# A count matrix relaid during the walk that sums it: 8 of 13 strip panels moved by quarters

## Chip, cores and metric

One core of one Trainium2 chip runs one program. The metric is the device time of one execution in microseconds (us). The kernel before took 4571.13 us (median of 3 runs, 4568.84 to 4574.15).

## The reference, cut to what matters

Four graph layers over 3125 nodes of 64 features and 103125 edges (sorted by destination). Layers 0, 2 and 3 are attention layers whose score depends on the two end nodes alone, so parallel edges weigh the same and all that is needed of the edges is how often each pair occurs:

```python
e = leaky_relu(s1[src] + s2[dst], 0.2)
m = segment_max(e, src); ex = exp(e - m[src])
att = ex / segment_sum(ex, src)[src]
h_prime = zeros.at[dst].add(att[:, None] * hW[src])
```

The kernel builds the matrix C[src, dst] of pair counts once (3200 x 3125, f32, in HBM) and layers 0, 2 and 3 read it. Layer 1 works edge by edge. This case is about how C gets to HBM.

## The kernel before, in words

**The walk.** The edges lie in groups of GE = 512, KE = 4 chunks of 128. The columns of C are cut into WN = 157 strips of WD = 20 destination nodes. A step handles one group against one strip, and there are SL = 360 steps, fixed ahead. A slot is the [128, 500] table of one step: row p is the low part of the source number, the 500 columns are 25 source blocks of 20 destinations. Per step:
- ACT (`distance`, L1100, four instructions, and `left`, L1107) makes the one-hot left operand, in four buffers `row_hot`, up to three steps ahead;
- DVE (`hot`, L1370, four compares of 500 columns, f16 in, bf16 out) makes the right operand `col_hot`, two steps ahead;
- PE (L768) multiplies, four matmuls into one bank;
- DVE (`total`, L1382) adds the bank to the running sum of the strip, multiplied by `keep` (0 where a new strip starts), into one of two flush buffers `fbuf` of four slots each.

After four steps SP (`flush`, L426) stores one buffer to `slots` in HBM, 90 flushes in all. `slots` has one row per (partition, step), and a partition's four slots of a flush lie together, 8000 bytes. In the first 17 pairs of flushes SP also stores zeros to `placed` (L434). The sum of a strip is whole in the last slot of its groups; `slot_i[:, w]` (L1342) is the row of `slots` where strip w's sum stands, for each partition.

**The relay, after the walk.** POOL (L637) waits until every flush has landed, then gathers strip after strip with an indirect DMA, [128, 500] each, 256 KB, 16 strips (WIDE) into one of two buffers `win`, ten panels. DVE (L1470) copies a panel in two halves (13 and 12 source blocks) from order strip-block to order block-strip into `relaid`; SP (L440) stores each half to the columns of C, in pieces of 16 x 20 x 4 = 1280 bytes. Between the panels POOL (L644) gathers rows of destinations, one per block of 128 nodes, with three buffers, and DVE (L1474) counts in them (NB = 25 counts, `row_counted`): a search for the first edge of every node. Each search b waits for count b - 3. Before the relay DVE prepares the row search (L1400 to L1416, `rows_ready`), weights (L1420 to L1429) and layer 0's node stage (`norm`, L1438 to L1447, and `proj`, L1455). After it come a few small operations (L1477 to L1490), a barrier over all five engines, and the first loads of C (L463) for layer 0.

Each engine works through its own list in order; semaphores link them. Indirect DMAs go by POOL and its own queue, all others here by SP.

Of the kernel before, what the change touches and what calls it, by code (L numbers as in the profile page):

```python
# [16 lines left out]
P = 128  # L17
N, D, E = 3125, 64, 103125
NB = -(-N // P)
# [17 lines left out]
PV = NB - 1 + -(-N // 512)  # L37
WIDE = 16
assert GN + WN - 1 <= SL and SL % 8 == 0
# [19 lines left out]
class Steps:  # L59
# [5 lines left out]
    def ran(self, ins):  # L65
        ins.then_inc(self.sem, 1)
        self.n += 1
# [23 lines left out]
def build(nc, x_in, src_in, dst_in, dst_before, dst_after, ea64, ea8, ew, w0, a0, gam, bet, wk1, wk2, wk3, wv1, wv2, wv3,  # L91
# [7 lines left out]
    c_cols = c_flat.rearrange("(b p f) o -> p b (f o)", b=NB, p=P)  # L99
    slots = nc.dram_tensor("slots", (P * SL, BW), F32).ap()  # L100
    slots_v = slots.rearrange("(p s) f -> p s f", p=P)
    mask_rows = nc.dram_tensor("mask_rows", (NB, P, N), BF16).ap()
# [9 lines left out]
    with ExitStack() as ctx:  # L112
        def sb(name, shape, dt=F32):
            return ctx.enter_context(nc.sbuf_tensor(name, shape, dt))

        def sem(name):
            return ctx.enter_context(nc.semaphore(name))
# [35 lines left out]
        arena = sb("arena", [P, ARENA])  # L153

        firstc = sb("firstc", [P, 2])
        lowest = sb("lowest", [P, 1])
# [22 lines left out]
        cb = Carve()  # L179
        cb.at = NP  # L180
        dgi, sgi, dgf, blki = (cb(2 * GE, t).rearrange("p (h n) -> p h n", h=2) for t in (I32, I32, F32, I32))
        lowf, keyf = (cb(2 * GE).rearrange("p (h n) -> p h n", h=2) for _ in range(2))
# [7 lines left out]
        chosen = [cb(SL) for _ in range(2)]  # L190
        base20, row0, keep = cb(SL), cb(1), cb(SL)
        last_dst, limit, limit_before, limit_end = cb(2, I32), cb(2), cb(2), cb(2)
        offset, outside, col_key = (cb(KE * SL).rearrange("p (k s) -> p k s", k=KE) for _ in range(3))
        minus_key = offset
        apart = [cb(KE * P, BF16) for _ in range(4)]
        iota16 = cb(COLS, F16)
        row_hot = [cb(KE * P, BF16) for _ in range(4)]
        col_hot = [cb(KE * BW, BF16) for _ in range(4)]
        assert cb.at <= cv.at
        cb.at = NP  # L200
        fbuf = [cb(4 * BW).rearrange("p (s f) -> p s f", s=4) for _ in range(2)]
        assert cb.at <= NP + 4 * 2 * GE
        cb.at = NP
        win = [cb(WIDE * BW) for _ in range(2)]
        relaid = [cb(13 * WIDE * WD) for _ in range(2)]
        assert cb.at <= cv.at
        big_m = cv(NP)
# [16 lines left out]
        tmp_n = sb("tmp_n", [P, NB, D])  # L224
        agg = sb("agg", [P, NB, D + 1])

# [81 lines left out]
        relaid_sb = sem("relaid_sb")  # L308
        relaid_out = [sem(f"relaid_out{i}") for i in range(2)]
        placed_zeroed, placed_out, seed_in = sem("placed_zeroed"), sem("placed_out"), sem("seed_in")  # L310
# [50 lines left out]
        def barrier(eng, k):  # L361

            eng.drain().then_inc(phase, 1)
            eng.wait_ge(phase, 5 * k)
# [6 lines left out]
        def fence(eng, go):  # L373

            eng.sem_inc(go, 1)

        block = ctx.enter_context(nc.Block())

# [8 lines left out]
        def _(sp):  # L387
# [33 lines left out]
            def flush(q, par):  # L421

                sp.wait_ge(summed, q * 4 + 4)
                if not isinstance(q, int):
                    fence(sp, sp_go)
                sp.dma_start(slots_v[:, bass.ds(q * 4, 4), :], fbuf[par]).then_inc(flushed[par], 16)  # L426

            for i in range(SL // 8):
                for par in range(2):
                    flush(i * 2 + par, par)  # L430
                lo = i * CROW
                if lo < W * D:
# [3 lines left out]
            for i in range(-(-WN // WIDE)):  # L436
                n = min(WIDE * WD, N - i * WIDE * WD)
                for half, (lo, nb) in enumerate(((0, 13), (13, 12))):
                    sp.wait_ge(relaid_sb, 2 * i + half + 1)
                    sp.dma_start(c_cols[:, lo:lo + nb, i * WIDE * WD:i * WIDE * WD + n],  # L440
                                 relaid[half][:, 0:nb * WIDE * WD].rearrange("p (b f) -> p b f", b=nb)[:, :, 0:n]).then_inc(relaid_out[half], 16)
            for half in range(2):
                sp.wait_ge(relaid_out[half], 16 * -(-WN // WIDE))
            barrier(sp, 1)
# [182 lines left out]
        def _(pool):  # L627

            for par in range(2):
                pool.wait_ge(flushed[par], 16 * (SL // 8))  # L630
            pool.wait_ge(placed_zeroed, 16 * -(-W * D // CROW))
            pool.wait_ge(table_out, 16)
            for i in range(-(-WN // WIDE)):
                if i >= 2:
                    pool.wait_ge(relaid_sb, 2 * i - 2)
                for w in range(i * WIDE, min(i * WIDE + WIDE, WN)):
                    pool.indirect_dma_start(out=win[i % 2][:, (w % WIDE) * BW:(w % WIDE + 1) * BW], out_offset=None, in_=slots,  # L637
                                            in_offset=bass.IndirectOffsetOnAxis(ap=slot_i[:, w:w + 1], axis=0)).then_inc(win_in[i % 2], 16)
                if i == 1:
                    pool.wait_ge(rows_ready, 1)  # L640
                for b in range(3 * i - 3, min(3 * i, NB)) if i else ():
                    if b >= 3:
                        pool.wait_ge(row_counted, b - 2)
                    pool.indirect_dma_start(out=found[b % 3], out_offset=None, in_=dst_in,  # L644
                                            in_offset=bass.IndirectOffsetOnAxis(ap=row_i[:, b:b + 1], axis=0)).then_inc(row_found[b % 3], 16)
            barrier(pool, 1)

# [648 lines left out]
        def _(dve):  # L1296
# [38 lines left out]
            dve.wait_ge(consts, 16)  # L1335
            ran(V.tensor_scalar(row0, nid[:, 0:1], float(SL), None, ALU.mult))
            ran(V.tensor_copy(out=sel[:, :, :], in_=cst[:, C_SEL:C_SEL + 4 * P].rearrange("p (j m) -> p j m", j=4)))
# [3 lines left out]
            V.tensor_tensor(base20, ps[7][:, 0:SL], iota20[:, 0:SL], ALU.add).then_inc(key_sb, 1)  # L1341
            V.scalar_tensor_tensor(slot_i[:, :], ps[6][:, 0:WN], row0, iota[:, 0:WN], ALU.add, ALU.add).then_inc(key_sb, 1)  # L1342
            dve.wait_ge(key_sb, 2)
# [29 lines left out]
            def total(s, j, n):  # L1373
# [10 lines left out]
                add.then_inc(summed, 1)  # L1384

            hot(0, 0)
            hot(1, 1)
# [3 lines left out]
            for i in range(SL // 8 - 2):  # L1391
                for j in range(8):
                    hot(i * 8 + (10 + j), (j + 2) % 4)
                    total(i * 8 + (8 + j), j, i * 16 + 16)
            for s in range(SL - 8, SL):
                if s + 2 < SL:
                    hot(s + 2, (s + 2) % 4)
                total(s, s % 8, 16 * (SL // 8 - 1))

            ran(V.tensor_scalar(diag0, ident, firstc[:, 0:1], None, ALU.mult))  # L1400
# [15 lines left out]
            do(V.tensor_copy(out=row_i[:, :], in_=row_f))  # L1416
            signal(rows_ready)

            dve.wait_ge(setup_a, 2)
# [37 lines left out]

            node_stage(0, 0)
            dve.wait_ge(brow_sb, NJ)


            for i in range(-(-WN // WIDE)):
                n = min(WIDE, WN - i * WIDE)
                dve.wait_ge(win_in[i % 2], 16 * (WIDE * (i // 2) + n))
                w4 = win[i % 2].rearrange("p (w b d) -> p b w d", w=WIDE, b=NB)
                for half, (lo, nb) in enumerate(((0, 13), (13, 12))):
                    if i:
                        dve.wait_ge(relaid_out[half], 16 * i)
                    o4 = relaid[half][:, 0:nb * WIDE * WD].rearrange("p (b w d) -> p b w d", b=nb, w=WIDE)
                    V.tensor_copy(out=o4[:, :, 0:n, :], in_=w4[:, lo:lo + nb, 0:n, :]).then_inc(relaid_sb, 1)  # L1470
                for b in range(3 * i - 3, min(3 * i, NB)) if i else ():
                    dve.wait_ge(row_found[b % 3], 16 * (b // 3 + 1))
                    at(row_counted, b, dve)
                    V.scalar_tensor_tensor(junk_b, found[b % 3], nid[:, b:b + 1], ones[:, 0:1].to_broadcast([P, W]),  # L1474
                                           ALU.is_le, ALU.mult, accum_out=cnt_in[:, b:b + 1]).then_inc(row_counted, 1)
            dve.wait_ge(row_counted, NB)
            do(V.scalar_tensor_tensor(cnt, row_f, float(W), cnt_in, ALU.mult, ALU.add))  # L1477
# [453 lines left out]
```

## Time and profile before

| | |
|---|---|
| median of the runs | 4571.13 us |
| the profiled execution | 4576.4 us, span 4574.6 us |
| DVE busy | 3821.1 us (84%) |
| PE busy | 3285.9 us (72%) |
| ACT busy | 2136.6 us (47%) |
| POOL busy | 1857.4 us (41%) |
| moved by DMA | 674.27 MB, mean 147 GB/s |
| L637, the strip gathers | x157, 171.6 us busy |
| L1370, the compares | x1440, 404.4 us busy |

Times in the rows are us from the span's start; busy is time in which the engine runs an instruction, and an instruction's duration can overlap the next one's on the same engine. A wait is put down to the event that came last. The walk takes the stretch from about 42 to 685 us, the relay the one from 690 to 973 us.

### The profile page before, as it was taken

How to read it: one execution, taken by the hardware profiler on the slowest of the kernel's cores; microseconds unless marked ns; L12 is line 12 of the kernel's file. 1: busy time of each engine (PE TensorE's matmuls, PEld its weight loads, DVE VectorE, ACT ScalarE, POOL GpSimd, SP SyncE). 2: the span in 40 equal slices, each digit the busy share in tenths (PEclk: the TensorE clock that was granted, in tenths of full speed). 3: DMA queues.
4: the chain of work that ended last, by engine and by line, in shares of the span. 5: the costliest groups of instructions: out<-in, count | busy, mean ns of one | idle time of the engine just before them, and what ended most of it. 6: DMA issues, size and time to landing. Idle time of an engine off the chain costs nothing. (4 is left out here: it accounts for less than half of the span.)

```text
span 4574.6 us, 66771 instructions
## 1 busy us (share of the span) xinstructions
PE 3285.9 (72%) x20105; PEld 1471.8 (32%) x20105; DVE 3821.1 (84%) x6803; ACT 2136.6 (47%) x4380; POOL 1857.4 (41%) x3682
## 2 busy tenths in 40 slices
PE   5555552016639999999994399999999998148166
PEld 2111111001214444444442144444444443122122
DVE  8999994359968888888888788888888886699898
ACT  6999990037723333334332144444444443057066
POOL 0000006720047777777762266666666665100000
PEclk9999995558769999999997699999999999579589
DMA  4653338986625555555551133333333332455544
GB/s 174 256 208 144 144 145 269 365 284 210 197 63 140 149 142 140 145 146 144 142 144 52 34 92 92 92 93 93 93 92 92 92 92 73 140 181 210 173 183 176
DMA packets 359857, 674.27 MB, mean 147 GB/s; under 512 B 71068, under 2 KB 261724, under 8 KB 347856
## 3 DMA queue, kind: packets, MB, share of 16 engines
q1 hardware_dynamic: 319824, 591.23, 39.0%
q0 software_dynamic: 39680, 78.78, 6.3%
q8 instruction: 167, 2.74, 0.3%
q14 instruction: 186, 1.52, 0.1%
HBM read 398.98 MB, written 270.79 MB: 146 GB/s over the span
## 5 line engine op out<-in xcount | busy, mean ns | idle before, releaser
L671 POOL DMA_INDIRECT arena<-h_table,gidx x808 | 785.1, 972 | 306.0 <-issue 229.4
L1635 DVE TENSOR_TENSOR arena<-banks,arena 128x512 f32<-128x512 f32 x808 | 536.2, 684 | 58.5 <-PE banks L861 38.9
L768 PE MATMUL banks<-arena 128*128 128x500 bf16 x1440 | 366.3, 376 | 278.2 <-DVE arena L1370 272.0
L1755 DVE TENSOR_TENSOR arena<-banks,arena 128x512 f32<-128x512 f32 x808 | 518.4, 683 | 37.2 <-PE banks L971 13.1
L1763 DVE TENSOR_TENSOR arena<-banks,arena 128x512 f32<-128x512 f32 x808 | 516.0, 680 | 1.3 <-PE banks L977 1.3
L1100 ACT ACTIVATE arena<-arena 128x128 bf16<-128x128 f16 x1440 | 455.8, 391 | 40.0 <-DVEq L1302 40.0
L637 POOL DMA_INDIRECT arena<-slots,slot_i x157 | 171.6, 1093 | 742.6 <-DMA slots<-arena 689.4
L1235 ACT ACTIVATE arena<-banks 64x256 f32<-64x256 f32 x808 | 306.0, 379 | 340.6 <-PE banks L1003 333.6
L991 PE MATMUL banks<-arena 128*64 128x256 f32 x3232 | 438.6, 392 | 0.5 <-DVE arena L1765 0.5
L977 PE MATMUL banks<-arena 64*128 64x512 f32 x1616 | 436.3, 617 | 0.9 <-DVE arena L1763 0.9
L867 PE MATMUL banks<-arena 128*64 128x256 f32 x3232 | 429.1, 387 | 0.0
L1370 DVE TENSOR_SCALAR arena<-arena 128x500 bf16<-128x500 f16 x1440 | 404.4, 345 | 0.1
L696 POOL TENSOR_TENSOR arena<-arena,same_prev 128x64 f32<-128x64 f32 x808 | 237.3, 294 | 394.4 <-ACT arena L1245 346.9
L819 PE MATMUL banks<-arena,proj 128*65 128x512 f32 (+1 forms) x700 | 277.3, 548 | 89.5 <-DVE arena L1837 89.5
L1171 ACT ACTIVATE arena<-banks 128x512 f32<-128x512 f32 x202 | 120.6, 597 | 404.6 <-PE banks L885 404.6
L867 PEld LDWEIGHTS banks<-arena 128*64 128x64 f32 x3232 | 214.7, 137 | 241.3 <-issue 91.2
L768 PEld LDWEIGHTS banks<-arena 128*128 128x128 bf16 x1440 | 117.4, 97 | 527.2 <-DVE arena L1370 439.9
L697 POOL TENSOR_TENSOR arena<-arena 128x64 f32<-128x64 f32 x808 | 259.2, 321 | 63.5
L819 PE MATMUL banks<-arena,lw 128*64 128x512 f32 (+1 forms) x350 | 182.2, 684 | 133.5 <-DVE lw L1527 133.5
L991 PEld LDWEIGHTS banks<-arena 128*64 128x64 f32 x3232 | 196.0, 136 | 246.0 <-DVE arena L1765 153.3
L1227 ACT ACTIVATE arena<-banks 128x256 f32<-128x256 f32 x202 | 77.6, 384 | 421.3 <-PE banks L993 421.3
L1382 DVE SCALAR_TENSOR_TENSOR arena<-arena,banks 128x500 f32<-128x500 f32 x359 | 263.5, 734 | 7.2 <-PE banks L768 1.0
(289 smaller groups left out, 6399.1 us busy)
## 6 DMA issues: line engine op xcount, KB each, us to landing
arena<-c_flat SPq DMA_DIRECT2D x75, 1562.5 KB, 6.8
slots<-arena SPq DMA_DIRECT2D x90, 1000.0 KB, 3.8
arena<-hs_dump SPq DMA_DIRECT2D x404, 128.0 KB
arena<-mask_rows SPq DMA_DIRECT2D x50, 781.2 KB, 4.3
arena<-in_edge_attr SPq DMA_DIRECT2D x202, 128.0 KB
arena<-placed SPq DMA_DIRECT2D x202, 128.0 KB
xs_dump<-arena SPq DMA_DIRECT2D x202, 128.0 KB
hs_dump<-arena SPq DMA_DIRECT2D x202, 128.0 KB
```

Source lines behind the costliest of these rows:

```text
L671: pool.indirect_dma_start(out=xs[par][:, k * D:(k + 1) * D], out_offset=None, in_=h_table, in_offset=bass.IndirectOffsetOnAxis(ap=gidx[par ...
L768: last = pe.matmul(ps[4 + r % 2][:, 0:BW], row_hot[r][:, k * P:(k + 1) * P], col_hot[r][:, k * BW:(k + 1) * BW], start=k == 0, stop=k == K ...
L819: last = pe.matmul(ps[j][0:rows, 0:n], proj[:, b, 2:rows + 2] if base else lw[par][:, :], ptile[par][:, j * COLS:j * COLS + n], start=b == ...
L867: last = pe.matmul(ps[7][k * D:(k + 1) * D, 0:TW // 2], k3[j], bt[j][:, k * (TW // 2):(k + 1) * (TW // 2)], start=j == 0, stop=j == 3)
L977: pe.matmul(ps[5 + j % 2][:, :], v3[j][rows, :], hv[t % 2][rows, :], start=True, stop=True).then_inc(y_ps, 1)
L991: last = pe.matmul(ps[2][k * D:(k + 1) * D, 0:TW // 2], wo[j], vt[j][:, k * (TW // 2):(k + 1) * (TW // 2)], start=j == 0, stop=False)
L1100: last = act.activation(apart[r % 4][:, k * P:(k + 1) * P], iota16[:, 0:P], ACT.Abs, bias=minus_key[:, k, bass.ds(s, 1)])
L1235: copied = act.activation(xat[r][half * D:(half + 1) * D, k * (TW // 2):(k + 1) * (TW // 2)], ps[0][k * D:(k + 1) * D, 0:TW // 2], ACT.Copy)
L1370: made = V.tensor_scalar(col_hot[r][:, k * BW:(k + 1) * BW], iota16[:, 0:BW], col_key[:, k, bass.ds(s, 1)], None, ALU.is_equal)
L1635: V.tensor_tensor(bt[j], ps[5 + j % 2][:, :], h2k[t % 2], ALU.mult).then_inc(bt_sb, 1)
L1755: V.tensor_tensor(dt_[j % 2], ps[3 + j % 2][:, :], xat[t % 3], ALU.mult).then_inc(dt_sb, 1)
L1763: V.tensor_tensor(vt[j], ps[5 + j % 2][:, :], dt_[j % 2], ALU.mult).then_inc(vt_sb, 1)
```

## The change

- Panels are of 12 strips instead of 16: 13 panels, the last of 13 strips. Each is copied and stored in four quarters of 7, 6, 6 and 6 source blocks, each quarter with its own buffer and semaphore. A stored piece is 12 x 20 x 4 = 960 bytes.
- Panels 0 to 7 are copied and stored during the walk: quarter i of panel g after step 4(58 + 4g + i) + 1, and its store by SP right behind flush 58 + 4g + i.
- POOL gathers three strips of a panel when flush 53 + 4g (then 54 + 4g, 55 + 4g, 56 + 4g) has landed, so panels 0 to 8 fall due within the walk and panel 9 to 12 after it. Panel 8 is copied right after the walk, panel 9 after `rows_ready`, panels 10, 11 and 12 between the counts, and the node stage of layer 0 stands between count 8 and panel 11.
- `slots` has its rows ordered step first, then partition, so that a gather can be bounded to the flushes that have landed; a flush writes four pieces of 2000 bytes per partition. `slot_i` takes two operations instead of one.
- Buffers move: `win` and `relaid` beside `fbuf` and `keep`; `row_hot`, `apart` and one `col_hot` into the space of `brow`; three `col_hot` into that of `big_m`; `offset` and `col_key` into `h` and `agg`.

```diff
-WIDE = 16
+WIDE = 12
+PANELS = WN // WIDE
+INSIDE = 8
+QUARTERS = ((0, 7), (7, 6), (13, 6), (19, 6))
...
-    slots_v = slots.rearrange("(p s) f -> p s f", p=P)
+    slots_v = slots.rearrange("(s p) f -> p s f", p=P)
...
+        def panel(g):
+            lo = g * WIDE
+            n = WIDE if g < PANELS - 1 else WN - lo
+            return lo, n, (GN - 1 + lo + n - 1) // 4
+        def copied_after(g, i):
+            return 4 * (58 + 4 * g + i) + 1
...
+            def store_panel(g, i):
+                lo, n, _ = panel(g)
+                cols = min(n * WD, N - lo * WD)
+                b, nb = QUARTERS[i]
+                sp.wait_ge(relaid_sb, 4 * g + i + 1)
+                sp.dma_start(c_cols[:, b:b + nb, lo * WD:lo * WD + cols],
+                             relaid[i][:, 0:nb * n * WD].rearrange("p (b f) -> p b f", b=nb)[:, :, 0:cols]).then_inc(relaid_out[i], 16)
+            stores = {copied_after(g, i) // 4: (g, i) for g in range(INSIDE) for i in range(4)}
             for i in range(SL // 8):
                 for par in range(2):
                     flush(i * 2 + par, par)
+                    if i * 2 + par in stores:
+                        store_panel(*stores[i * 2 + par])
...
+            def landed(q):
+                pool.wait_ge(flushed[0], 16 * (q // 2 + 1))
+                pool.wait_ge(flushed[1], 16 * ((q + 1) // 2))
+            def gather_panel(g):
+                lo, n, _ = panel(g)
+                if g >= 2:
+                    pool.wait_ge(relaid_sb, 4 * g - 4)
+                for w in range(lo, lo + n):
+                    q = min(max((GN - 1 + lo + n - 1) // 4, 53 + 4 * g + (w - lo) // 3), SL // 4 - 1)
+                    if (w - lo) % 3 == 0:
+                        landed(q)
+                    pool.indirect_dma_start(out=win[g % 2][:, (w - lo) * BW:(w - lo + 1) * BW], out_offset=None, in_=slots[0:(q + 1) * 4 * P, :],
+                                            in_offset=bass.IndirectOffsetOnAxis(ap=slot_i[:, w:w + 1], axis=0)).then_inc(win_in[g % 2], 16)
...
+            for g in range(INSIDE + 3):
+                gather_panel(g)
+            pool.wait_ge(placed_zeroed, 16 * -(-W * D // CROW))
+            pool.wait_ge(table_out, 16)
+            pool.wait_ge(rows_ready, 1)
+            find_rows(0, 3)
+            gather_panel(INSIDE + 3)
+            find_rows(3, 9)
+            gather_panel(INSIDE + 4)
+            find_rows(9, NB)
...
+            def copy_panel(g, i):
+                lo, n, _ = panel(g)
+                dve.wait_ge(win_in[g % 2], 16 * (WIDE * (g // 2) + n))
+                if g:
+                    dve.wait_ge(relaid_out[i], 16 * g)
+                w4 = win[g % 2][:, 0:n * BW].rearrange("p (w b d) -> p b w d", w=n, b=NB)
+                b, nb = QUARTERS[i]
+                o4 = relaid[i][:, 0:nb * n * WD].rearrange("p (b w d) -> p b w d", b=nb, w=n)
+                V.tensor_copy(out=o4, in_=w4[:, b:b + nb, :, :]).then_inc(relaid_sb, 1)
...
                     hot(i * 8 + (10 + j), (j + 2) % 4)
                     total(i * 8 + (8 + j), j, i * 16 + 16)
+                    if i * 8 + 8 + j in copies:
+                        copy_panel(*copies[i * 8 + 8 + j])
...
+            for i in range(4):
+                copy_panel(INSIDE, i)
...
             signal(rows_ready)
+            for i in range(4):
+                copy_panel(INSIDE + 1, i)
...
+            count_rows(0, 6)
+            for i in range(4):
+                copy_panel(INSIDE + 2, i)
+            count_rows(6, 9)
+            node_stage(0, 0)
+            for i in range(4):
+                copy_panel(INSIDE + 3, i)
+            count_rows(9, 15)
+            for i in range(4):
+                copy_panel(INSIDE + 4, i)
+            count_rows(15, NB)
```

`find_rows` and `count_rows` hold the two loop bodies that stood between the panels before (L644, L1474).

## Rows read from the trace of the kernel before

**Rows 1.** Busy us by stretch: PE, PEld, DVE, ACT, POOL; granted clock, DMA share, GB/s

```profile
44.00:50.00 6.00, 4.74 (x12) 1.31 (x12) 4.14 (x14) 6.00 (x18) 0.00 (x0) 0.50 0.00 0
...
460.00:660.00 200.00, 113.94 (x452) 36.66 (x452) 198.08 (x564) 200.00 (x563) 0.00 (x0) 1.00 0.35 145
740.00:960.00 220.00, 0.00 (x0) 0.00 (x0) 84.19 (x67) 0.00 (x0) 157.59 (x147) 0.50 1.03 356
```

**Rows 2.** Timeline, start and duration in us: the walk's last sums, C's first loads

```profile
683.55 1.59 DVE L1382 SCALAR_TENSOR_TENSOR arena<-arena,banks 128x500 f32<-128x500 f32 x2 [1.05 <-PE banks L768]
...
972.94 2.25 SPq L463 DMA_DIRECT2D arena<-c_flat  x4
```

**Rows 3.** Waits from 686 to 1000 us: in total, times, longest

```profile
DVE arena L1470 <- DMA arena<-slots,slot_i: 88.1, 7, 15.4
```

**Rows 4.** Timeline of DVE just after the walk's start

```profile
50.59 0.73 DVE L1382 SCALAR_TENSOR_TENSOR arena<-arena,banks 128x500 f32<-128x500 f32 x1
51.23 1.12 DVE L1370 TENSOR_SCALAR arena<-arena 128x500 bf16<-128x500 f16 x4
...
55.64 0.73 DVE L1382 SCALAR_TENSOR_TENSOR arena<-arena,banks 128x500 f32<-128x500 f32 x1
```

**Rows 5.** Groups by line and shape, 686 to 990 us

```profile
L1470 DVE COPY arena<-arena 128x4160 f32<-128x4160 f32 x9 | 40.4, 4486 | 97.3 <-DMA arena<-slots,slot_i 75.0 <-DMA c_flat<-arena 11.6 <-ACT arena L1086 10.8
L1474 DVE SCALAR_TENSOR_TENSOR arena<-arena,cst,ones 128x808 bf16<-128x808 int32 x25 | 26.5, 1061 | 1.7
...
L1470 DVE COPY arena<-arena 128x3840 f32<-128x3840 f32 x9 | 19.7, 2190 | 33.6 <-DMA c_flat<-arena 33.6
...
L1470 DVE COPY arena<-arena 128x3380 f32<-128x3380 f32 x1 | 2.1, 2054 | 13.1 <-DMA arena<-slots,slot_i 13.1
```

**Rows 6.** Gathers beside DVE: all casts of L1583, then the timeline, twice

```profile
L1583 DVE CAST arena<-arena x26: 411/420/640, 1314.1 to 2339.8; 128x512 bf16<-128x512 f32 x26
...
2143.69 0.95 POOL L671 DMA_INDIRECT arena<-h_table,gidx  x1 [0.30 <-issue]
...
2144.18 0.16 DVE L1629 COPY gidx<-srci 128x4 int32<-128x4 int32 x1
2144.25 0.64 DVE L1583 CAST arena<-arena 128x512 bf16<-128x512 f32 x1
...
860.72 2.16 DVE L1470 COPY arena<-arena 128x3840 f32<-128x3840 f32 x1 [1.94 <-DMA c_flat<-arena]
861.04 2.66 POOL L637 DMA_INDIRECT arena<-slots,slot_i  x1 [0.30 <-issue]
```

**Rows 7.** DMA queues (packets, MB, share of 16 engines) at 300:600, then 760:940

```profile
q1 hardware_dynamic: 6048, 43.01, 34.6%
...
q0 software_dynamic: 8568, 36.23, 53.8%
q1 hardware_dynamic: 23098, 29.26, 50.1%
```

**Rows 8.** The flushes of the walk (59 to 683 us), landing after issue

```profile
DMA to landing us min/median/max: 3.8/3.8/4.2
```

**Rows 9.** The strip gathers: durations, first and last start, landing after issue

```profile
L637 POOL DMA_INDIRECT arena<-slots,slot_i x157: 942/947/3118, 689.8 to 950.1; - x157
...
DMA to landing us min/median/max: 3.4/6.3/11.9
```

**Rows 10.** Timeline of DVE after the walk

```profile
699.55 1.82 DVE L1438 TENSOR_REDUCE stat<-x 128x25 f32<-128x1600 f32 x1
...
726.04 0.43 DVE L1455 COPY proj<-banks 128x264 f32<-128x264 f32 x1 [1.07 <-PE banks L801]
...
964.55 0.18 DVE L1477 SCALAR_TENSOR_TENSOR cnt<-row_f,cnt_in 128x25 f32<-128x25 f32 x1
...
967.80 0.18 DVE L1490 CAST start_i<-cnt 128x25 int32<-128x25 f32 x1
```

More of the change, by code:

```diff
@@ L99, in build @@
     c_cols = c_flat.rearrange("(b p f) o -> p b (f o)", b=NB, p=P)
-    slots = nc.dram_tensor("slots", (P * SL, BW), F32).ap()
-    slots_v = slots.rearrange("(p s) f -> p s f", p=P)
+    slots = nc.dram_tensor("slots", (SL * P, BW), F32).ap()
+    slots_v = slots.rearrange("(s p) f -> p s f", p=P)
     mask_rows = nc.dram_tensor("mask_rows", (NB, P, N), BF16).ap()
@@ L153, in build @@
         arena = sb("arena", [P, ARENA])
+        agg = sb("agg", [P, NB, D + 1])
         firstc = sb("firstc", [P, 2])
@@ L180, in build @@
         cb.at = NP
+        fbuf = [cb(4 * BW).rearrange("p (s f) -> p s f", s=4) for _ in range(2)]
+        iota16 = cb(COLS, F16)
+        keep = cb(SL)
+        panels_at = cb.at
         dgi, sgi, dgf, blki = (cb(2 * GE, t).rearrange("p (h n) -> p h n", h=2) for t in (I32, I32, F32, I32))
@@ L190, in build @@
         chosen = [cb(SL) for _ in range(2)]
-        base20, row0, keep = cb(SL), cb(1), cb(SL)
+        base20, last_step = cb(SL), cb(WN)
         last_dst, limit, limit_before, limit_end = cb(2, I32), cb(2), cb(2), cb(2)
-        offset, outside, col_key = (cb(KE * SL).rearrange("p (k s) -> p k s", k=KE) for _ in range(3))
+        outside = cb(KE * SL).rearrange("p (k s) -> p k s", k=KE)
+        offset, col_key = (v[:, :, :].rearrange("p b f -> p (b f)")[:, 0:KE * SL].rearrange("p (k s) -> p k s", k=KE) for v in (h, agg))
         minus_key = offset
+        assert cb.at <= cv.at
+        cb.at = panels_at
+        win = [cb((WIDE + 1) * BW) for _ in range(2)]
+        relaid = [cb(nb * (WIDE + 1) * WD) for _, nb in QUARTERS]
+        assert cb.at <= cv.at
+        cb.at = 0
         apart = [cb(KE * P, BF16) for _ in range(4)]
-        iota16 = cb(COLS, F16)
         row_hot = [cb(KE * P, BF16) for _ in range(4)]
[L198 to L206, printed above, removed]
+        col_hot = [cb(KE * BW, BF16)]
+        assert cb.at <= NP
+        cb.at = cv.at
+        col_hot += [cb(KE * BW, BF16) for _ in range(3)]
+        assert cb.at <= cv.at + NP
         big_m = cv(NP)
@@ L224, in build @@
         tmp_n = sb("tmp_n", [P, NB, D])
-        agg = sb("agg", [P, NB, D + 1])
         diag0, frow = (agg[:, :, :].rearrange("p b f -> p (b f)")[:, i * P:(i + 1) * P] for i in range(2))
@@ L308, in build @@
         relaid_sb = sem("relaid_sb")
-        relaid_out = [sem(f"relaid_out{i}") for i in range(2)]
+        relaid_out = [sem(f"relaid_out{i}") for i in range(4)]
         placed_zeroed, placed_out, seed_in = sem("placed_zeroed"), sem("placed_out"), sem("seed_in")
@@ L434, in _ @@
                     sp.dma_start(placed_v[:, lo:lo + n], zeros[:, 0:n]).then_inc(placed_zeroed, 16)
[L436 to L443, printed above, removed]
+            for g in range(INSIDE, PANELS):
+                for i in range(4):
+                    store_panel(g, i)
+            for i in range(4):
+                sp.wait_ge(relaid_out[i], 16 * PANELS)
             barrier(sp, 1)
@@ L627, in _, with find_rows @@
         def _(pool):
[L629 to L641, printed above, removed]
+            def landed(q):
[11 more added lines that the diff above has]
+                                            in_offset=bass.IndirectOffsetOnAxis(ap=slot_i[:, w:w + 1], axis=0)).then_inc(win_in[g % 2], 16)
+            def find_rows(lo, hi):
+                for b in range(lo, hi):
                     if b >= 3:
@@ L1335, in _ @@
             dve.wait_ge(consts, 16)
-            ran(V.tensor_scalar(row0, nid[:, 0:1], float(SL), None, ALU.mult))
             ran(V.tensor_copy(out=sel[:, :, :], in_=cst[:, C_SEL:C_SEL + 4 * P].rearrange("p (j m) -> p j m", j=4)))
@@ L1341, in _ @@
             V.tensor_tensor(base20, ps[7][:, 0:SL], iota20[:, 0:SL], ALU.add).then_inc(key_sb, 1)
-            V.scalar_tensor_tensor(slot_i[:, :], ps[6][:, 0:WN], row0, iota[:, 0:WN], ALU.add, ALU.add).then_inc(key_sb, 1)
+            do(V.tensor_tensor(last_step, ps[6][:, 0:WN], iota[:, 0:WN], ALU.add))
+            V.tensor_scalar(slot_i[:, :], last_step, float(P), nid[:, 0:1], ALU.mult, ALU.add).then_inc(key_sb, 1)
             dve.wait_ge(key_sb, 2)
@@ L1384, in total @@
                 add.then_inc(summed, 1)
+            def copy_panel(g, i):
[7 more added lines that the diff above has]
+                V.tensor_copy(out=o4, in_=w4[:, b:b + nb, :, :]).then_inc(relaid_sb, 1)
+            copies = {copied_after(g, i): (g, i) for g in range(INSIDE) for i in range(4)}
+            assert max(copies) < SL
             hot(0, 0)
@@ L1398, in _ @@
                 total(s, s % 8, 16 * (SL // 8 - 1))
+                if s in copies:
+                    copy_panel(*copies[s])
+            for i in range(4):
+                copy_panel(INSIDE, i)
             ran(V.tensor_scalar(diag0, ident, firstc[:, 0:1], None, ALU.mult))
@@ L1456, in node_stage, with count_rows @@
                 dve.wait_ge(proj_sb, 4 * (k + 1))
[L1458 to L1471, printed above, removed]
+            def count_rows(lo, hi):
+                for b in range(lo, hi):
                     dve.wait_ge(row_found[b % 3], 16 * (b // 3 + 1))
@@ L1475, in _ @@
                                            ALU.is_le, ALU.mult, accum_out=cnt_in[:, b:b + 1]).then_inc(row_counted, 1)
+            count_rows(0, 6)
[3 more added lines that the diff above has]
+            node_stage(0, 0)
+            for i in range(4):
+                copy_panel(INSIDE + 3, i)
+            count_rows(9, 15)
+            for i in range(4):
+                copy_panel(INSIDE + 4, i)
+            count_rows(15, NB)
+            dve.wait_ge(brow_sb, NJ)
             dve.wait_ge(row_counted, NB)
```

## The prediction

> **What bounds the kernel now.** First the busy time by stretch [rows 1]. In the walk (about 42 to 685 us) ACT and DVE are both full (200.00 and 198.08 of 200 us) and the DMA engines work at 0.35 once the zeros are written; from 740 to 960 us PE and ACT do nothing, DVE is busy 84 of 220 us, and the DMA engines are full at 356 GB/s. That second stretch is what the count matrix costs after the walk: from the end of the walk's last sum (683.55 + 1.59 = 685.1 us) to the first load of the matrix at 972.9 us [rows 2] it is 287.8 us, nothing of layer 0 can start before it ends, and the longest waits of its copies are for gathers (88.1 us) [rows 3]. So a strip moved while the walk has free DMA time is gained, and what it costs the walk has to be paid on DVE.
>
> Who paces the walk? In steady state ACT runs 562 instructions in its full 200 us [rows 1], five to a step: 1.78 us. Just after the start DVE is behind and runs alone: of four sums in a row the first starts at 50.59 and the last at 55.64, 1.68 us apart each, of which 1.12 go to the compares [rows 4]. So a step costs ACT 1.78 us and DVE 1.68; DVE has 0.10 us a step to give, and ACT, which may be three steps ahead, hides nothing more.
>
> **Part 1: copies in the walk.** 32 quarter copies go in, one per four steps. Prices [rows 5]: 4160 elements took 4.49 us (1.04 ns each behind a fixed 0.15), 3840 took 2.19 (0.52 ns behind 0.19). The slow form has 13 blocks into a target without gaps; the last panel's 3380 elements, also 13 blocks but into a target with gaps, took 2.05, the fast rate. A quarter of 7 blocks (1680 elements, no gaps) is nearest to the slow row: 1.90 us (fast: 1.06); a quarter of 6 (1440) is even like 12: 0.91 us. The Trainium skill (VectorE: DVE Perf Modes, Mode 2×_2P) says two ports serve a copy if the outermost dimensions are both even, or odd and equal; these rows agree, and by it the 7-block quarter is slow too. A panel is 1.90 + 3 x 0.91 = 4.63 us, eight are 37.1 us. From the first copy (after step 233) to step 359 DVE has 127 steps x 0.10 = 12.4 us to give. Net +24.7 us (least, with the 7-block quarter fast, +18).
>
> **Part 2: gathers beside DVE.** In the walk DVE's one-hot compare takes 1.12 of 1.68 us for four times 500 columns [rows 4], about half of what the slow copy needs per element, so it is taken to use both ports. No gather ran beside it; the nearest rows are layer 1's casts beside gathers [rows 6]. A gather began at 2143.69, the cast at 2144.25 took 0.64 us where the median is 0.42 and ended 0.78 + 0.42 us after the gather's start; the small copy that began at 2144.18, 0.49 us after it, took its usual 0.16. So a gather shuts DVE out of the two-port forms from about 0.54 to 0.78 us after its start: 0.24 us at most. With the compare there 1.1 of 1.68 us, a gather costs about 0.64 x 0.24 + 0.01 = 0.165 us; about 108 gathers (panels 0 to 8) fall into the walk: +18 us, between 0 (DVE's queued compares go first) and 26. The other way round, a gather that began at 861.04 under a two-port copy took 2.66 us in place of 0.95: it ended 0.82 us after the copy [rows 6]. Under compares I take one gather per 1.3 to 1.75 us in place of 1.25; three per flush take 4 to 5.2 us, which fits into four steps.
>
> The rule that speaks against the change: the Trainium skill (SBUF — State Buffer, Who interferes with whom) says that the port pair which DVE and GpSimd share is locked for the whole instruction of whoever came first. What the sum would be by it is the second rival below; the copy at 2144.18, inside a gather and not slowed, speaks against it.
>
> **Part 3: transfers in the walk.** Per flush there are now 1.02 MB of flush in pieces of 2000 B (before 8000), 0.77 MB of gathers, and on average 0.77 MB of stores in pieces of 960 B (before 1280). From 760 to 940 us a hardware packet (29.26 MB in 23098, 50.1% of 16 x 180 us) took 62 ns for 1267 B; in the walk (43.01 MB in 6048, 34.6% of 16 x 300 us) 275 ns for 7112 B [rows 7]: 16 ns + 0.036 ns per byte. That makes 2.85 us for the flush, 2.57 for a store and, at the gathers' own 53.8% of 16 x 180 us for 36.23 MB, 2.05 us: 7.5 us. The period is 4 x 1.68 + 1.16 + 3 x 0.165 = 8.4 us. 89% full: it fits, with queueing. A flush landed 3.8 us after issue [rows 8], a gather 3.4 us at least and 6.3 in the median, mostly in the full stretch [rows 9]. Quarter 0 of a panel is copied six steps after the flush that its last three strips need is issued: 6 x (1.68 + 0.14) + 0.91 = 11.8 us. Needed: flush 4.5 to 6, third gather issued 2.5 to 3.5 later, landing 3.4 to 6.3: 10.4 to 15.8 us, middle about 12.8. One us of waiting per panel, +8 us, between 0 and 32. The flush buffers are not late (four steps plus a copy against 4 to 6 us), nor are the targets of the copies (four flushes). SP has nothing else in its queue there, and each store stands behind a flush whose sums come later than the copy. The walk gets **24.7 + 18 + 8 = 51 us** longer (18 to 95).
>
> **Part 4: after the walk.** Left are 49 gathers, 61 strips to store, 25 row searches. Clock from the walk's end, durations as before [rows 5, 9, 10]:
> - panel 8's last gathers (flush 88) land at 4; copied 4 to 9;
> - DVE's set-up (685.1 to 699.5 before, 14.4 us; its search part ends 2 us earlier) 9 to 23; row searches may start;
> - POOL gathers panel 9 from 4 to 24 (12 x 1.25 us, 0.95 and the 0.31 between two [rows 6, 9], held up by the copies and by two-input operations), panel 10 to 41; panel 9 is copied 28 to 33;
> - searches 0 to 2 are issued by 45, counted by 50; panel 11's gathers to 61, searches 3 to 5 counted by 70 (DVE takes its work in order and waits from 35 on, save for the counts); panel 10 copied by 75, counts 6 to 8 by 79;
> - node stage (699.55 to 726.5 before, 27 us) to 106; panel 11 copied by 110, counts 9 to 14 by 120; panel 12 by 125;
> - ten more counts. Search b waits for count b - 3, so three take one landing and one count, 4.5 + 1.2 us: 1.9 us each, to 145. Before, the closing operations took 964.55 to 967.98, 3.4 us, and the load came 5 us later, with the last store, which now has long landed; 3.4 us and the barrier: **150 us**.
> Transfers: 12.5 + 15.6 + 10.3 = 38.4 MB at 356 GB/s are 108 us, so they no longer bind; searches and DVE's order do. Bounds 130 (no wait before the node stage) and 170. Gain 287.8 - 150 = 138 us. The one added operation before the walk costs 0.3 us; slot numbers and buffers moved elsewhere cost nothing.
>
> **Sum.** 51 - 138 = -87 us. The profiled execution took 4576.4 us (span 4574.6); the median of the runs is 5.3 us lower. 4576.4 - 87 - 5 = **4485 us**.
>
> **Rivals.** (a) Nearly all costs absent: locks lost to DVE's queue, no landing late: walk +20, tail 140: about 4443. For it: casts that don't start in that quarter of a microsecond keep their median [rows 6], and a flush landed within 4.2 us at most [rows 8]. 12%. (b) A gather blocks a compare for its whole 0.95 us: 108 x 0.6 x 0.95 = 62 us in place of 18, and later gathers: about 4535. Against it rows 6. 10%. (c) The DMA engines become the bound of the walk: if 960 B pieces and 2000 B pieces cost half as much again, the flush takes 10 us against 8.4, 34 times 1.7 us, and landings are late by 3 us a panel: +82, about 4567. For it: 89% by my own sum. 8%. (d) **Slower**: POOL starves. If a gather has to wait for a gap between the compares twice (once to read its indices, once to write), and each time until the next step, it takes more than two steps. Twelve gathers have 16 steps and four copies, 33 us per panel. A panel's 16 steps took 28.5 us before, so the change loses from 28.5 + 138 / 9 = 44 us per panel on, 3.7 us per gather; at 4 us per gather it is 48 us, +175 us in the walk: about 4608. For it: 1.7 us of delay from a single copy [rows 6]; against it: sums leave 0.6 us of every step free, and the reads come within the first 0.1 us. 4%. (e) The change doesn't do what it says: panels are copied so late that part of the eight still lie behind the walk; each costs there 12 x 1.66 us (157 gathers from 689.8 to 950.1 us [rows 9]): two panels, +40, about 4525. 6%. The forecast itself, 4455 to 4515, has 60%.
>
> A change of PE's clock is no term: from 44 to 50 us the granted clock was 0.50 (1.2 GHz) and 12 matmuls made PE busy for 4.74 us [rows 1], 1.58 us a step and still under 1.68.
>
> **Numbers.** Range 4443 to 4545: it leaves out part of (a), (c) and (d). About 0.2% (9 us) is what a measurement here can tell from no change. Faster 0.93, same 0.02, slower 0.05, from (d), part of (c), and what I haven't seen.
>
> **What the profile would show.** Right: copies of 1680 elements near 1.9 us and of 1440 near 0.9; the walk's period 8.4 us per flush from step 233; compares' mean a few tens of ns up; DMA at 0.9 there; the matrix's first load about 150 us after the last sum; waits of the copies for gathers about 1 us each. Wrong: gathers over 2.5 us in the walk (d), sums waiting for flushes (c), the row searches hiding less or more than the tail above.

## The result, and the profile after

The changed kernel took 4517.38 us (median of 4 runs, 4509.15 to 4524.02) against 4572.64 us (4 runs) before: the ratio is 0.9876, 95% interval 0.9864 to 0.9889, 55 us less. The profiled execution took 4518.56 us, its span is 4516.8. The forecast was 87 us less and 4485 us, with a range of 4443 to 4545.

The trace splits the difference in two. Timeline of the changed kernel, the walk's last sums and the first loads of C, as [rows 2]:

```profile
754.22 1.56 DVE L1428 SCALAR_TENSOR_TENSOR arena<-arena,banks 128x500 f32<-128x500 f32 x2
...
913.80 2.32 SPq L492 DMA_DIRECT2D arena<-c_flat  x4
```

The walk ends at 755.8 us (before 685.1: 70.6 longer, forecast 51), and from there to the first load it is 158.0 us (before 287.8: 129.8 shorter, forecast 138). -130 + 71 = -59 us, and the span is 58 us shorter.

Busy time by stretch, as [rows 1] (the last stretch is the one behind the walk):

```profile
461.00:700.00 239.00, 122.47 (x404) 36.04 (x402) 198.63 (x525) 185.59 (x516) 81.19 (x75) 0.81 0.84 268
...
756.00:914.00 158.00, 27.63 (x101) 19.51 (x101) 75.57 (x115) 7.68 (x15) 84.43 (x77) 0.52 0.88 265
```

From step 233 on the walk no longer fills DVE: 198.63 of 239 us, where it had been full [rows 1]. The missing 40 us stand in the groups of DVE by shape for the same stretch, as [rows 5]: name, count, busy time, mean ns, and idle time before:

```profile
L1416 DVE TENSOR_SCALAR arena<-arena,agg 128x500 bf16<-128x500 f16 x400 | 114.7, 347 | 0.0
L1428 DVE SCALAR_TENSOR_TENSOR arena<-arena,banks 128x500 f32<-128x500 f32 x100 | 72.3, 723 | 0.0
L1441 DVE COPY arena<-arena 128x1440 f32<-128x1440 f32 x18 | 16.2, 898 | 0.0
L1441 DVE COPY arena<-arena 128x1680 f32<-128x1680 f32 x7 | 13.3, 1903 | 40.4 <-DMA arena<-slots,slot_i 40.4
```

All of it lies before the first quarter of a panel (the only one of 1680 elements), and a gather ends it each time. Over the whole walk it is this row of the waits from 412 to 756 us (in total, times, longest):

```profile
DVE arena L1441 <- DMA arena<-slots,slot_i: 44.9, 8, 7.3
```

So the walk's 70 us from step 233 on (294.0 us from the start of that step's sum to the end, before 224.1) are 36.8 us of copies, 44.9 us of waiting, and -11.8 us that are left for the steps: the spare time that DVE had (forecast 12.4). One wait in the timeline, panel 1:

```profile
486.57 0.36 SPq L445 DMA_DIRECT2D slots<-arena  x1
...
492.96 1.48 POOL L671 DMA_INDIRECT arena<-slots,slot_i  x1 [3.63 <-DMA slots<-arena]
...
494.29 0.36 SPq L445 DMA_DIRECT2D slots<-arena  x1
494.70 0.51 SPq L453 DMA_DIRECT2D c_flat<-arena  x1
494.74 0.95 POOL L671 DMA_INDIRECT arena<-slots,slot_i  x1 [0.31 <-issue]
...
496.00 1.05 POOL L671 DMA_INDIRECT arena<-slots,slot_i  x1 [0.30 <-issue]
...
497.09 0.72 DVE L1428 SCALAR_TENSOR_TENSOR arena<-arena,banks 128x500 f32<-128x500 f32 x1
...
504.09 1.90 DVE L1441 COPY arena<-arena 128x1680 f32<-128x1680 f32 x1 [6.28 <-DMA arena<-slots,slot_i]
```

The flush is issued at 486.6 and releases POOL at 493.0; the third gather starts at 496.0, and the copy that waits for it starts 8.1 us later. The next flush and a store, 1.8 MB together, had been issued just ahead of the second gather. That is 17.5 us from the flush to the copy; DVE was there 6.3 us earlier.

The other panels look alike. In panels 1 to 6 the flush landed 6.1 to 8.0 us after its issue, the third gather started 2.8 to 3.3 us after that, and it took 7.2 to 7.6 us to land (panels 2, 4 and 6; the trace has no landings for the odd ones); the copy started 16.9 to 18.4 us after the flush. In panel 0 it was 14.1 us, in panel 7 15.4.

The stretch's mean of 0.84 for the DMA engines hides that they are full during the wait and half empty behind it (columns as in [rows 1]). In seven of the eight waits their share is 0.93 to 1.05, in panel 0's 0.63:

```profile
490.00:498.00 8.00, 5.59 (x17) 1.59 (x18) 7.80 (x22) 7.50 (x21) 3.48 (x3) 0.79 1.03 337
498.00:504.00 6.00, 0.96 (x4) 0.24 (x4) 0.00 (x0) 3.70 (x11) 2.08 (x3) 0.78 1.03 327
504.00:512.00 8.00, 4.19 (x11) 1.25 (x12) 7.91 (x21) 2.27 (x6) 0.76 (x1) 0.52 0.47 151
```

A flush now lands later, too. Landing after issue of all flushes, 402 to 756 us, against 3.8/3.8/4.2 in [rows 8] (4.1/4.2/4.6 in the changed kernel from 60 to 400 us, before the first gather):

```profile
DMA to landing us min/median/max: 4.1/5.8/8.0
```

Behind the walk DVE waits for row searches (`in_dst,row_i`) and POOL for DVE's counts (waits, 756 to 914 us), as [rows 3]:

```profile
DVE arena L1531 <- DMA arena<-in_dst,row_i: 48.4, 9, 12.7
POOL arena L679 <- DVE arena L1531: 37.7, 7, 12.2
DVE arena L1441 <- DMA arena<-slots,slot_i: 15.3, 2, 10.9
```

### The profile page after: what moved, and what is told of

The parts are those of the page before. It is cut to its first block and busy times, and to the rows that moved or that the text cites. A ratio compares the mean times of both kernels' runs of the same rounds, so it can differ in the third digit from the quotient of the medians.

```text
span 4516.8 us, 66927 instructions
## 1 busy us (share of the span) xinstructions
PE 3314.6 (73%) x20105; PEld 1476.7 (33%) x20105; DVE 3811.3 (84%) x6835; ACT 2140.0 (47%) x4380; POOL 1859.1 (41%) x3682
## 5 line engine op out<-in xcount | busy, mean ns | idle before, releaser
L814 PE MATMUL banks<-arena 128*128 128x500 bf16 x1440 | 392.3, 400 | 321.9 <-DVE arena L1416 177.0
L1146 ACT ACTIVATE arena<-arena,h 128x128 bf16<-128x128 f16 x1440 | 454.9, 388 | 40.8 <-DVEq L1348 40.8
L1416 DVE TENSOR_SCALAR arena<-arena,agg 128x500 bf16<-128x500 f16 x1440 | 407.9, 346 | 0.1
L1153 ACT ACTIVATE arena<-arena,ones 128x512 bf16<-128x512 bf16 x360 | 255.3, 709 | 61.4 <-PE banks L814 61.1
```

What stands on the lines that cost most here:

```text
L814: last = pe.matmul(ps[4 + r % 2][:, 0:BW], row_hot[r][:, k * P:(k + 1) * P], col_hot[r][:, k * BW:(k + 1) * BW], start=k == 0, stop=k == K ...
L1146: last = act.activation(apart[r % 4][:, k * P:(k + 1) * P], iota16[:, 0:P], ACT.Abs, bias=minus_key[:, k, bass.ds(s, 1)])
L1416: made = V.tensor_scalar(col_hot[r][:, k * BW:(k + 1) * BW], iota16[:, 0:BW], col_key[:, k, bass.ds(s, 1)], None, ALU.is_equal)
```

## The experiments

Theory A: what the walk loses is lateness, a chain of flush, three gathers and their landing that is longer than the six steps it has. Theory B: it is bandwidth, so that moving the gathers only moves the wait. e2 to e6 are single runs, so of them stretches and waits are read rather than times. The runs of e4, e6 and e7_all were made on a chip on which the kernel took some 500 us longer, the one before too (5102.52 us), most of it in layer 1. The three edits together (e7) ran on both chips: the walk ended at 706.5 us there and at 705.2 here, and the stretch behind it took 153.8 and 148.5 us. So behind the walk some 5 us between the two chips say nothing.

**e1: gathers one flush earlier.**

```diff
-                    q = min(max((GN - 1 + lo + n - 1) // 4, 53 + 4 * g + (w - lo) // 3), SL // 4 - 1)
+                    q = min(max((GN - 1 + lo + n - 1) // 4, 52 + 4 * g + (w - lo) // 3), SL // 4 - 1)
```

> The gathers of every panel but the first are issued one flush earlier (from flush 52 + 4g on instead of 53 + 4g); nothing else. Theory A, lateness: in the changed kernel quarter 0 of each panel waits 5.6 us because its last gathers come out 17.4 us after the flush they need, and the copy 11.9 us after it. One flush earlier gives 8.2 us more, so the waits of panels 1 to 7 fall to 0, panel 0 keeps its 3.5 us; the period of a panel falls from 37.6 to about 32 us, the walk gets about 41 us shorter and the kernel 4476 us. Theory B, bandwidth: a panel's 10 MB need 37 us of the DMA engines with these pieces; the wait moves to the flush buffers or to the stores and the period stays above 36 us, the kernel above 4505 us.

4474.31 us against 4575.62 before, ratio 0.9779 (0.9761 to 0.9796). The groups of DVE in the same stretch:

```profile
L1416 DVE TENSOR_SCALAR arena<-arena,agg 128x500 bf16<-128x500 f16 x480 | 137.7, 347 | 0.0
L1428 DVE SCALAR_TENSOR_TENSOR arena<-arena,banks 128x500 f32<-128x500 f32 x120 | 86.7, 722 | 1.1 <-DMA slots<-arena 1.1
L1441 DVE COPY arena<-arena 128x1440 f32<-128x1440 f32 x22 | 20.1, 912 | 0.0
L1441 DVE COPY arena<-arena 128x1680 f32<-128x1680 f32 x8 | 15.1, 1890 | 0.0
```

120 sums lie in the stretch instead of 100, and no copy waits. Panel 0's does not either: the edit moves its last nine strips too, which the expectation overlooked. The last sum ends at 711.7 us, 44.1 earlier; behind it 155.2 us pass (158.0 before the edit). A holds: the time came out within 2 us of what it asked for, 30 below what B did. B is not far, though: the same stretch has the DMA engines at 0.99, and for the first time a sum waits for a flush (1.1 us):

```profile
461.00:700.00 239.00, 146.83 (x484) 43.16 (x484) 237.90 (x630) 221.92 (x618) 108.70 (x90) 0.86 0.99 318
```

**e2: copies two steps later.**

```diff
-            return 4 * (58 + 4 * g + i) + 1
+            return 4 * (58 + 4 * g + i) + 3
```

> Copies two steps later (after step 4(58 + 4g + i) + 3), gathers as in the changed kernel. A: two more steps are 3.4 us, so the waits fall from 5.6 to 2.2 us a panel, the walk gets 25 us shorter, perhaps less as each store now comes later behind its flush. B: waits unchanged at over 5 us a panel.

One run, 4488.1 us. The copies waited 14.1 us in all (seven of eight panels, 1.5 to 3.1 us each), 30.8 less, and the walk ended at 725.3 us, 30.4 earlier. This is A's arithmetic: two more steps, 3.4 us, took 4 us off each wait.

**e3: no stores in the walk.** The 32 stores are made behind it.

```diff
                     flush(i * 2 + par, par)
-                    if i * 2 + par in stores:
-                        store_panel(*stores[i * 2 + par])
...
-            for g in range(INSIDE, PANELS):
+            for g in range(PANELS):
...
-                if g:
+                if g >= INSIDE:
                     dve.wait_ge(relaid_out[i], 16 * g)
```

> The 32 stores to the count matrix leave the walk: they are made after it, from whatever stands in the buffers then, so the first eight panels of the matrix hold wrong counts and the time after the walk is longer and is not read. A says what makes the gathers late is queueing behind a flush and a store in a row: without the store a flush lands in about 4.5 us instead of 6, the third gather in 4 to 5 instead of 8, needed 4.5 + 3.3 + 4.5 = 12.3 us against 11.9: waits under 1 us a panel and a period of 32 us. If POOL's own pace beside DVE were what is late, the waits would stay above 3 us a panel.

One run, 4596.24 us, in which the first eight panels of the matrix hold wrong counts. Waits of the copies from 412 to 770 us, and the flushes' landing from 461 to 700 us:

```profile
DVE arena L1439 <- DMA arena<-slots,slot_i: 29.7, 8, 4.2
...
DMA to landing us min/median/max: 4.1/6.0/6.4
```

The waits stayed at 3.7 us a panel, where under 1 was expected, and a flush landed as late as with the stores (6.0 us from 461 to 740 us in the changed kernel). What fell was the third gather's landing, to 5.3 to 6.0 us in panels 1 to 7. So the stores make up a third of the waiting, and it is not they that make a flush late.

By the expectation, waits above 3 us would have meant that POOL's own pace was late. The trace says otherwise: the third gather started 3.1 to 3.4 us after the flush had landed, where three gathers with nothing in their way need 2.5 (two periods of 1.25 us). That is at most 0.9 us of the 3.7.

**e5: two panels gathered, the rest copied from the same buffers.**

```diff
-            for g in range(INSIDE + 3):
+            for g in (0, 1, *range(INSIDE, INSIDE + 3)):
                 gather_panel(g)
...
-                dve.wait_ge(win_in[g % 2], 16 * (WIDE * (g // 2) + n))
+                dve.wait_ge(win_in[g % 2], 16 * (WIDE * max(g // 2 - INSIDE // 2 + 1, 0) + n))
```

> Only panels 0 and 1 are gathered in the walk; panels 2 to 7 are copied and stored from those same buffers, so their counts are wrong. From panel 2 on no gather runs beside DVE. Price of the shared port: a step between copies took 1.705 us in the changed kernel and 1.683 where DVE ran alone, so if only the port is at work it falls to 1.683 to 1.685, 3 us over 127 steps, not the 18 us predicted nor the 62 of the whole-instruction lock. Waits of the copies are 0 and the period is 16 x 1.684 + 4.6 = 31.5 us; with stores and flushes left, a flush should land in about 4.2 to 5 us.

Groups of DVE from 461 to 700 us, and the flushes' landing in the same stretch:

```profile
L1416 DVE TENSOR_SCALAR arena<-arena,agg 128x500 bf16<-128x500 f16 x467 | 131.1, 341 | 0.0
...
L1441 DVE COPY arena<-arena 128x1680 f32<-128x1680 f32 x8 | 15.2, 1894 | 9.3 <-DMA arena<-slots,slot_i 9.3
...
DMA to landing us min/median/max: 4.2/4.3/6.5
```

One run, 4482.89 us, with wrong counts as well. Without gathers a flush lands in 4.3 us beside the stores: the gathers cost it the 1.7 us. The 9.3 us of waiting are those of panels 0 and 1, which were gathered.

And the price of gathers beside DVE can be read: a compare takes 341 ns in the mean against 347 with gathers, and the steps between copies (94 of them, by the starts of their sums) 1.678 us against 1.705. Over 127 steps that is 3.4 us for some 100 gathers, 0.03 us each. A count of the lengthened compares in the changed kernel gives the same size: from 461 to 700 us 33 of 398 took over 0.36 us, 2.8 us more in all than the usual 0.34 each, beside 75 gathers. In e1, where DVE never waits for a copy, it was 38 of 480, 3.7 us beside 90 gathers. The steps themselves scatter by about as much (1.687 us in e2, 1.726 in e1), so the price is 0.03 to 0.04 us and no finer.

**e4: the 7-block quarter with gaps in its target.**

```diff
-                             relaid[i][:, 0:nb * n * WD].rearrange("p (b f) -> p b f", b=nb)[:, :, 0:cols]).then_inc(relaid_out[i], 16)
+                             relaid[i][:, 0:nb * (WIDE + 1) * WD].rearrange("p (b f) -> p b f", b=nb)[:, :, 0:cols]).then_inc(relaid_out[i], 16)
...
-                o4 = relaid[i][:, 0:nb * n * WD].rearrange("p (b w d) -> p b w d", b=nb, w=n)
+                pitch = WIDE + 1
+                o4 = relaid[i][:, 0:nb * pitch * WD].rearrange("p (b w d) -> p b w d", b=nb, w=pitch)[:, :, 0:n, :]
```

> Only the copies' target changes: blocks stand 13 strips apart instead of 12, so the target of a 7-block quarter has gaps and keeps three dimensions like its source. If the slow form comes from the dimensions (13 blocks without gaps 4.49 us, 13 blocks with gaps 2.05), 1680 elements fall from 1.90 to about 1.06 us, 8 times 0.84 us in the walk, where part of it may turn into longer waits for the gathers, and 4 times after it: 3 to 10 us in all. If the size or the odd count alone makes it slow, 1.90 stays.

```profile
L1442 DVE COPY arena<-arena 128x1440 f32<-128x1440 f32 x19 | 17.0, 897 | 0.0
L1442 DVE COPY arena<-arena 128x1680 f32<-128x1680 f32 x7 | 8.1, 1164 | 40.1 <-DMA arena<-slots,slot_i 40.1
```

It takes 1.16 us in place of 1.90, with the same size and the same odd count: the target's dimensions make it slow. The walk ended 5.8 us earlier, as 8 x 0.74 us asks for; behind it 162.8 us passed (158.0), which is within what the two chips differ by.

**e6: node stage before the first counts.**

```diff
-            count_rows(0, 6)
+            node_stage(0, 0)
+            count_rows(0, 3)
             for i in range(4):
                 copy_panel(INSIDE + 2, i)
-            count_rows(6, 9)
-            node_stage(0, 0)
+            count_rows(3, 6)
             for i in range(4):
                 copy_panel(INSIDE + 3, i)
-            count_rows(9, 15)
+            count_rows(6, 12)
...
-            find_rows(3, 9)
+            find_rows(3, 6)
             gather_panel(INSIDE + 4)
-            find_rows(9, NB)
+            find_rows(6, NB)
```

> After the walk only the order changes: DVE does layer 0's node stage (27 us) before the first counts, copies panel 11 before counts 6 to 11, and POOL gathers panel 12 before search 6. In the changed kernel DVE stood idle 12.7 and 12.1 us before counts 0 and 3 and the whole took 158.0 us from the last sum to the first load. If DVE's order is the bound there, that falls to about 140 us. If it is the searches (25, three in flight, behind gathers and stores), it stays within 5 us of 158.

From the last sum to the first load 156.4 us passed, against 158.0. By the expectation, 140 would have made DVE's order the bound, and it wasn't; a gain of a few us is not excluded, since the two runs are of different chips. DVE's waits for searches fell from 48.4 to 28.3 us, and 14.9 us of waits for stores came instead.

**e7: the edits of e1, e4 and e6 together**, on both chips.

> The three edits together: gathers one flush earlier, gapped copies, node stage first. Walk as with the early gathers (last sum at 711.7 us) less 8 x 0.84 = 705 us; after it 155 less 18 less 4 = 133 us; the kernel about 4474 - 29 = 4445 us if the parts add up; over 4465 us if the DMA engines, now near full, take the copies' gain back.

> The same kernel as the three edits together, beside the one above on the same chip: last sum at about 706.5 us, first load 154 us later.

4975.54 us against 5102.52, ratio 0.9749 (0.9724 to 0.9774), on the chip with the longer layer 1, and 4458.04 us against 4574.31, ratio 0.9747 (0.9734 to 0.9761), on the other. Last sum at 706.5 and 705.2 us, as expected; behind it 153.8 and 148.5 us, not 133. Against e1 that is some 15 us, half of the 29 that were to add up.

**e8: e7 with six row searches in flight.**

```diff
+        found += [fbuf[i % 2].rearrange("p s f -> p (s f)")[:, i // 2 * W:(i // 2 + 1) * W].bitcast(I32) for i in range(3)]
...
-                    if b >= 3:
-                        pool.wait_ge(row_counted, b - 2)
+                    if b >= 6:
+                        pool.wait_ge(row_counted, b - 5)
```

The waits of searches and counts on their buffers get six semaphores instead of three, and the order follows: counts 0 to 5, the copies of panels 10 and 11, counts 6 to 11; on POOL the searches 0 to 5 stand ahead of the gathers of panel 11, 6 to 11 ahead of those of panel 12.

> The three edits together plus six row searches in flight in place of three (three more buffers in the flush buffers' space) and DVE copying panels 10 and 11 in a row. Node stage first alone left the time after the walk at 156 us, so the order of DVE's work isn't its bound. If the searches' depth is (9 to 10 us per three of them while stores and gathers fill the DMA engines), the time from last sum to first load falls from 154 to about 135 us and the kernel by 18 us against the three edits. If the transfers are (38.4 MB at 356 GB/s, 108 us, and near 1.0 of the engines in most of it), it falls by less than 8 us.

4445.64 us against 4574.31 before, ratio 0.9722 (0.9709 to 0.9736), and 12.4 us under e7 on the same chip. Behind the walk 134.0 us passed against 148.5; that is 14.5 us less, between the 18 and the 8 us of the expectation. The stretch behind the walk of e8, then of e7:

```profile
704.00:838.00 134.00, 24.58 (x101) 16.65 (x101) 73.67 (x115) 7.56 (x15) 82.17 (x74) 0.53 0.97 308
```

```profile
705.00:854.00 149.00, 27.44 (x101) 19.05 (x101) 73.13 (x116) 7.78 (x15) 84.82 (x75) 0.51 0.91 276
```

DVE's waits for searches and for stores in the same stretches, e8's, then e7's:

```profile
DVE arena L1443 <- DMA c_flat<-arena: 31.9, 7, 8.2
...
DVE arena L1533 <- DMA arena<-in_dst,row_i: 4.1, 1, 4.1
```

```profile
DVE arena L1532 <- DMA arena<-in_dst,row_i: 37.3, 14, 8.7
...
DVE arena L1442 <- DMA c_flat<-arena: 10.8, 3, 3.9
```

The waits for searches are all but gone, though a search took longer to land (8.7 us in the median against 6.3): the searches in flight were what bound this stretch. e8 also moves the copies of panel 11 and the gathers of panels 11 and 12 among the searches, and the share of that in the 14.5 us was not measured apart. Behind it stand the stores: the waits for them grew to 31.9 us, and the DMA engines are at 0.97. This kernel is the fastest of all: 128.7 us under the one before, where the change had come out 55.3 under it.

## Why the forecast was right in kind and short in size

**What bounded the kernel**: right. The walk's free DMA time was there to be used, and what was done in it came off the stretch behind.

**The sum**: -87 forecast, -59 measured in the trace. It lies this near partly by luck, since the two largest errors point opposite ways: 15 us too much for the gathers beside DVE (part 2), 37 too little for the waits (part 3). With part 2 right and all else as forecast, it would have been 4470 us and 47 off. Part 4 was 8 us short.

**Part 1, copies**: right to 1%. 1680 elements took 1.90 us, 1440 took 0.90, in all 36.8 us (forecast 37.1). DVE's spare time was there: the steps gave back 11.8 us, the price of the gathers already taken off.

**Part 2, gathers beside DVE**: the kind right, the size not: 3 us measured (e5) where 18 stood. The step that failed is "a gather costs about 0.64 x 0.24", which takes the most that one gather cost a cast for what each gather costs: 75 gathers lengthened 33 compares, by 0.08 us each in the mean. Rival (b), in which a gather blocks a compare for its whole 0.95 us, would have added 62 us and is refuted for these gathers. It is the whole-instruction lock of the Trainium skill (SBUF — State Buffer, Who interferes with whom); this trace does not agree, with 3 us. POOL paid a little: of the 75 gathers 33 took over 1.0 us, the longest 1.90, where the median stayed at 0.95, and the starts of three lay 3.0 us apart in the timeline above in place of 2.5.

**Part 3, transfers**: this is the term that was mis-sized most, 45 us where 8 stood. The chain was set up as needed, but two of its three links came out above their own bounds: "landing 3.4 to 6.3" was 7.2 to 7.6 us, and the flush, "4.5 to 6", took 6.1 to 8.0 in panels 1 to 6. The gathers' issue lay within its bounds (2.8 to 3.3), and the time that the copy gave was 11.2 us instead of 11.8. The rows for the landing came from gathers with stores or alone, none from gathers issued right behind a 1 MB flush and a 0.8 MB store; the flush had been measured with no gather beside it at all. e1 and e2 show the lateness by giving it time, e3 and e5 who makes it: gathers delay the flush by 1.7 us, stores are a third of the waiting. How much of the last link the flush ahead of it makes, no run shows.

The mean load was no guide to this. It was near what had been forecast, 89% (0.84 with the waits in it), and so was the price of a packet of the flushes and stores; queues from 420 to 740 us, as [rows 7]:

```profile
q1 hardware_dynamic: 41938, 57.93, 52.1%
q0 software_dynamic: 6336, 25.35, 29.5%
```

That is 64 ns for 1381 bytes, where 16 ns + 0.036 ns per byte give 66. The gathers' part came out dearer, 29.5% of 16 x 320 us for 25.35 MB: 2.9 us of all engines per flush where 2.05 stood. Rival (c), dearer small pieces, did not come in, and over the walk the engines had room, which e1 then used. The room was not where the chain needed it: 0.93 to 1.05 of the engines in seven of the eight waits, 0.47 from 504 to 512 us.

**Part 4, behind the walk**: 158 for 150 us. By its own clock: panel 8 copied at 15 instead of 9 us after the last sum (its gathers were late in the same way), counts 3 to 5 at 70 (70), panel 10 at 75 (75), node stage at 105 (106), panel 12 at 130 (125), last count at 154 (145). "Searches and DVE's order" as the bound was half right: e6 changed the order and gained next to nothing, e8 gave the searches depth and gained 14.5 us.

**PE's clock** fell in the walk: 0.81 granted from 461 to 700 us, a mixture of stretches at 1.2 and at 2.4 GHz, where it had been 1.00. From 474 to 490 us it was 1.00; in the wait from 498 to 504 us PE was busy for 0.96 of 6 us, and from 504 to 512 us the clock was 0.52. The waits are not all of it, since e1, which has none, still shows 0.86; what else lowers it stays open. It cost nothing that shows: in e1 DVE is full all the same.

**Rivals** (a), (d) and (e) did not happen: the walk got 71 us longer and not 20, gathers stayed under 2 us, and all eight panels were copied within the walk.

## What to carry to other kernels

When work is moved beside a loop, write out the chain from the last transfer that it needs to its consumer, and price each link with what stands in front of it in the queues at that moment, not with its duration elsewhere; then start the producer one round earlier than the sum says. A mean load under 1 does not say that a transfer lands in time: here the DMA engines were at 0.84 in the mean and at 0.93 or more in seven of the eight waits. One digit, 53 to 52, was worth 43 us. Behind the loop look at the buffer depth of small gathers as well as at the order of the work: where a search took 3.7 to 11 us to land, three in flight kept DVE waiting for 37 us and six for 4.

## What the runs showed of the hardware

- A gather issued behind a flush and a store took 7 to 8.8 us to land, 3.1 to 3.7 us with little else in the queues. A flush took 4.3 us with stores and no gathers (e5), 6.0 with gathers and no stores (e3). The gathers are in flight when the flush is issued, the store stands behind it, so this compares their places as well as their kinds.
- Beside indirect DMAs from POOL, DVE's compares lose 0.03 to 0.04 us per gather. The delay belongs to a part of the gather alone: of the 52 casts of one shape in layer 1 before (26 of them in [rows 6]), the nine that started 0.53 to 0.75 us after a gather took 0.45 to 0.66 us, the other 43 took 0.41 to 0.47.
- A copy in the fast form with an odd number of blocks takes the time of the larger half: 7 blocks of 240 took 1.16 us, four of them being 960 elements; the last panel's 13 blocks of 260 took 2.05 [rows 5], seven being 1820. Both are 0.16 us and 1.04 ns for each element of that half; by an equal half of 840 it would have been 1.03 us.
- The same 7 blocks took 1.90 us when they touched in the target, which the trace then shows as one run of 1680 elements, and 1.16 with a gap between them (e4).
- The walk with early gathers (e1) moved 318 GB/s at 0.99 of the DMA engines, in pieces of 960 and 2000 bytes; in pieces of 1280 and 2000 it had been 356 at 1.03 [rows 1].
